# One reduction over four terms in place of three multiply-adds, in an RK4 step on one Trainium2 core

## The chip, the cores and the metric

The kernel runs on one core of a Trainium2 chip. The metric is the device time of one execution in microseconds. Three executions of the kernel before gave 6045.94, 6048.6 and 6047.53 us; their median, 6047.53 us, is the time before. TensorE multiplies matrices, VectorE (DVE in the profile) and ScalarE (ACT) work element by element on 128 partitions, GpSimd (POOL) only fills constants here, and SyncE (SP) issues the transfers. Each engine has its own queue of instructions and works through it in order; between engines, and for a result on the same engine, semaphores order the work.

## The reference

Two layers follow one another. The first is one attention head over `x` of shape (8, 512, 1024); it takes under a tenth of the time and the change doesn't touch it. The second integrates 512 time steps with the classical fourth-order Runge-Kutta scheme and adds the trace of `q` to its input:

```
def _derivative(q, p, drive, coupling, bias):
    i_couple = jnp.tanh(q) @ coupling.T
    dq = q - q ** 3 / 3.0 - p + drive + i_couple + bias
    dp = EPSILON * (q + ALPHA - BETA * p)
    return (dq, dp)

def _rk4_step(q, p, drive, coupling, bias):
    dq1, dp1 = _derivative(q, p, drive, coupling, bias)
    dq2, dp2 = _derivative(q + 0.5 * DT * dq1, p + 0.5 * DT * dp1, drive, coupling, bias)
    dq3, dp3 = _derivative(q + 0.5 * DT * dq2, p + 0.5 * DT * dp2, drive, coupling, bias)
    dq4, dp4 = _derivative(q + DT * dq3, p + DT * dp3, drive, coupling, bias)
    q_next = q + DT / 6.0 * (dq1 + 2 * dq2 + 2 * dq3 + dq4)
    p_next = p + DT / 6.0 * (dp1 + 2 * dp2 + 2 * dp3 + dp4)
    q_next = jnp.clip(q_next, -CLAMP, CLAMP)
    p_next = jnp.clip(p_next, -CLAMP, CLAMP)
    return (q_next, p_next)
...
drive_tbn = jnp.swapaxes(input_drive_seq, 0, 1)
```

The state `q` is 8 rows (batch) of 1024 values, the coupling is 1024 x 1024, and each of the 4 stages of a step needs the whole `q` of the stage before. So the second layer is a chain of 512 x 4 = 2048 stages, each with one product of an 8 x 1024 matrix by a 1024 x 1024 one.

## The kernel before

**Layout.** The 1024 values lie as 8 blocks of 128 partitions, so `q` is a tile of 128 x 64 (8 blocks times 8 rows of the batch). All tiles of the state are slices of one buffer, and the profile calls each of them `xb`. The blocks form two chunks: chunk 0 has 3 blocks (24 columns), chunk 1 has 5 (40 columns). The tanh and the coupling are each split into a high and a low half-precision part; the tanh's parts are called FIRST and REST. FIRST comes from a forecast or from the tanh itself, REST is what is missing from it.

**One stage.** A stage `s` goes round the engines in this order:

1. TensorE (line 604) multiplies, and its results lie in `ps`. It begins when FIRST and REST of chunk 0 are there (`first_ready[0]`, `rest_ready[0]`), and goes on to its second half when those of chunk 1 are. It signals `product_done[0]`, and after the last matmuls `product_done[1]`.
2. VectorE transposes the product of each chunk into `turned_sums` (`turn_product`, line 796; 96 columns for chunk 0, 160 for chunk 1).
3. VectorE adds the REST product to what was prepared (`q_of`): `q_next = turned_sum * step_scale + base`. `step_scale` is a column of one value for each partition, since the coupling was scaled by its own power of two.
4. ScalarE takes the tanh of that chunk (`tanh`, line 422), VectorE makes REST out of it (`rest_of`, seen as `tanh_parts<-xb,tanh_parts`), and TensorE starts the next stage.

**The prepared part.** `base` is made on VectorE between stages: `with_first_part` adds the product of FIRST, scaled by `step_scale`, to the linear terms; ScalarE squares the new `q` (line 466); `cubic_of` (line 819) makes `(q*q - 3) * q`; `base_of` adds that, scaled, to the rest.

**Order.** Nothing is scheduled by a program: `stage(s, now)` lists VectorE's instructions by hand, with the work for `p` and the linear terms placed between the links of the chain. Nearly all multiply-adds are made by one helper, `axpy`, and have its line, 646. In stage 0 and stage 2 ScalarE also forecasts the tanh of the stage after next (line 434, copied at line 440), and where the next stage is odd it copies the tanh to FIRST (line 428). VectorE's loop holds two steps, 8 stages, and branches back (line 1035) behind the last work of a stage 0. In stage 3, `clip_p` (914), `clip_q` (928) and `drive_less_p` (923) stand ahead of the second `rest_of`.

Of the kernel before, what the change touches and what calls it, by code (L numbers as in the profile page):

```python
# [17 lines left out]
P = 128  # L18
# [58 lines left out]
TANH_SCALE = 4096.0  # L77
COUP_EXP = 14
DRIVE_LOADS = 8
# [5 lines left out]
def build(nc, x, x_pt, cond, cond_p, wq, wk, wv, wo, coupling_t, bias_p, out_pt):  # L85
    ctx = ExitStack()
    with ctx:
# [18 lines left out]

        turned_sums = sb("turned_sums", [P, NC, SQ])
# [34 lines left out]
        step_scale = sb("step_scale", [P, STAGES])  # L142
# [13 lines left out]
        cubic = state()  # L156
        base = state()
        z = state()
        z2 = state()
        z3 = state()  # L160
        z_first_part = state()
# [17 lines left out]
        z_rest = state()  # L179

# [64 lines left out]
        cubic_ready = sem("cubic_ready")  # L245
        base_ready = sem("base_ready")

        z_ready = sem("z_ready")
        z_rest_ready = sem("z_rest_ready")
# [106 lines left out]
        def _(act):  # L356
# [68 lines left out]
            def first_part_as_now(parity, j, count):  # L425

                act.wait_ge(tanh_ready[j], count)
                nc.scalar.activation(tanh_part(parity, j, FIRST), by_block(tanh_sb, CHUNKS[j]), ACT.Copy,  # L428
                                     scale=TANH_SCALE).then_inc(first_ready[j], 1)

            def first_part_from_forecast(parity, factor, forecasts, made):

                act.wait_ge(forecast_ready, forecasts)
                nc.scalar.activation(tanh_hat[:, :], forecast[:, :], ACT.Tanh, scale=factor)\  # L434
# [4 lines left out]
                for j in range(NCH):  # L439
                    nc.scalar.activation(tanh_part(parity, j, FIRST), by_block(tanh_hat, CHUNKS[j]), ACT.Copy,  # L440
                                         scale=TANH_SCALE).then_inc(first_ready[j], 1)

            for j in range(NCH):
                tanh(q_st[0], j, 1)
            for j in range(NCH):
                act.wait_ge(tanh_ready[j], 1)
                nc.scalar.activation(tanh_part(1, j, FIRST), by_block(tanh_sb, CHUNKS[j]), ACT.Copy,
                                     scale=TANH_SCALE).then_inc(start_ready, 1)
            for j in range(NCH):
                first_part_as_now(0, j, 1)  # L450
            nc.scalar.activation(square[:, :], q_st[0][:, :], ACT.Square).then_inc(square_ready, 1)

            with act.Fori(1, 1 + STAGES * STEPS, STAGES * UNROLLED) as now:
                for u in range(STAGES * UNROLLED):
                    s = u % STAGES
                    following = (s + 1) % STAGES
                    parity = following % 2
                    made = act.snap(now + 1)
                    q = q_st[following] if following else q_raw
                    for j in range(NCH):  # L460
                        tanh(q, j, made)
                        if following % 2 == 1:
                            first_part_as_now(parity, j, made)
                    if following == 0:
                        act.wait_ge(clipped, act.snap(now >> 2))
# [175 lines left out]
        def _(dve):  # L641
# [98 lines left out]
            V.tensor_scalar(all_max[:, :], small_ps[:, 0:1], 2.0 ** -100, 2.0 ** 100, ALU.max, ALU.min)\  # L740
# [31 lines left out]
            V.tensor_copy(q_st[0][:, :], cond_sb[:, :, :].rearrange("p c b -> p (c b)"))  # L772
# [301 lines left out]
```

## Time and profile before

| | |
|---|---|
| median of three executions | 6047.53 us |
| the profiled execution | 6057.33 us, of which the span is 6055.5 us |
| VectorE busy | 5678.5 us, 94% of the span |
| TensorE busy (matmul) | 4516.8 us, 75% |
| ScalarE busy | 2596.6 us, 43% |
| mean granted TensorE clock | 0.995 of full speed |
| the 2048 stages | 430.5 us to the end |

A busy share counts the time in which at least one instruction of the engine is under way. Successive VectorE instructions overlap at their ends: one begins before the one ahead has written its last result. So a duration is one thing (when the result is there for another engine) and the distance from one start to the next is another (when the queue is free for the next). Both are used below. Starts stand in the timeline, to 0.01 us.

### The profile page before, as it was taken

To read this page: it belongs to the slowest core of one execution; us is meant where nothing else is said; L and a number is where in the kernel's file an instruction comes from. 1 tells how busy PE (TensorE), PEld (TensorE's weight loads), DVE (VectorE), ACT (ScalarE), POOL (GpSimd) and SP (SyncE) were. 2 spreads that over 40 slices of the span, in tenths; PEclk is the share of its full clock that TensorE was granted. 3 is DMA by queue.
4 is the path that set the end of the run, shared out by engine and by line. 5 is a ranking of instruction groups with operands and counts; after the bars stand their busy time and mean duration, and the time that the engine had idled before them with its cause. 6 is when DMAs were issued, how large, how long until landed. Compare 5 with 4: busy or idle time off the path is not lost.

```text
span 6055.5 us, 592967 instructions
## 1 busy us (share of the span) xinstructions
PE 4516.8 (75%) x263627; PEld 3815.0 (63%) x263627; DVE 5678.5 (94%) x32584; ACT 2596.6 (43%) x12040; POOL 5.6 (0%) x16
## 2 busy tenths in 40 slices
PE   7887777777777777777777777777777777777777
PEld 3446666666666666666666666666666666666666
DVE  5569999999999999999999999999999999999999
ACT  3334444444444444444444444444444444444444
POOL 0000000000000000000000000000000000000000
PEclk8999999999999999999999999999999999999999
DMA  5100000000000000000000000000000000000000
GB/s 206 44 15 0 0 7 0 7 0 7 0 0 7 0 7 0 7 0 0 7 0 7 0 7 0 0 7 0 7 0 7 0 0 7 0 7 0 7 0 7
DMA packets 11597, 57.06 MB, mean 9 GB/s; under 512 B 2616, under 2 KB 2616, under 8 KB 8512
## 3 DMA queue, kind: packets, MB, share of 16 engines
q1 hardware_dynamic: 11056, 55.84, 2.3%
q10 hardware_dynamic: 528, 1.05, 0.0%
q8 instruction: 7, 0.11, 0.0%
q14 instruction: 6, 0.05, 0.0%
HBM read 40.11 MB, written 16.78 MB: 9 GB/s over the span
## 4 chain that ended last, share of the span: by engine, by line
DVE 81%; issue 8%; ACT 5%; PE 5%; DVEq 1%; DMA 0%; SPq 0%; ACTq 0%
DVE xb L646 44%; DVE turned_sums L796 14%; DVE tanh_parts L646 8%; ACT xb L422 5%; DVE xb L819 5%; DVE xb L855 2%; DVE xb L923 2%; PE ps L493 2%; DVE drive L934 1%; DVE xb L908 1%; DVE xb L884 1%; PE ps L511 1%; DVE xb L914 1%; PE ps L548 1%; PE ps L537 1%
## 5 line engine op out<-in xcount | busy, mean ns | idle before, releaser
L604 PE MATMUL ps<-coup,tanh_parts 128*16 128x96 f16 (+1 forms) x262272 | 4165.0, 219 | 1463.9 <-ACT tanh_parts L428 740.9
L604 PEld LDWEIGHTS ps<-coup,tanh_parts 128*16 128x16 f16 x262272 | 3652.9, 89 | 1976.6 <-ACT tanh_parts L428 924.5
L422 ACT ACTIVATE xb<-xb 128x24 f32<-128x24 f32 (+1 forms) x4098 | 940.4, 230 | 3091.9 <-DVE xb L646 3081.7
L646 DVE SCALAR_TENSOR_TENSOR xb<-xb 128x64 f32<-128x64 f32 x11267 | 2153.5, 214 | 70.0
L646 DVE SCALAR_TENSOR_TENSOR xb<-turned_sums,step_scale,xb 128x64 f32<-128x64 f32 (+2 forms) x6145 | 1561.2, 261 | 41.7 <-issue 0.4
L796 DVE STREAM_TRANSPOSE turned_sums<-ps 128x96 f32<-128x96 f32 (+1 forms) x4096 | 1281.5, 313 | 70.4 <-issue 69.1
L646 DVE SCALAR_TENSOR_TENSOR tanh_parts<-xb,tanh_parts 128x24 f16<-128x24 f32 (+1 forms) x4098 | 717.1, 175 | 15.6
L466 ACT ACTIVATE xb<-xb 128x64 f32<-128x64 f32 x2048 | 499.3, 244 | 0.0
L428 ACT ACTIVATE tanh_parts<-xb 128x24 f16<-128x24 f32 (+1 forms) x2050 | 471.1, 230 | 64.5
L819 DVE SCALAR_TENSOR_TENSOR xb<-xb 128x64 f32<-128x64 f32 x2049 | 450.8, 220 | 0.1
L440 ACT ACTIVATE tanh_parts<-xb 128x24 f16<-128x24 f32 (+1 forms) x2048 | 357.3, 221 | 32.2
L434 ACT ACTIVATE xb<-xb 128x64 f32<-128x64 f32 x1024 | 263.4, 257 | 0.0
L855 DVE TENSOR_TENSOR xb<-xb 128x64 f32<-128x64 f32 x1024 | 225.9, 221 | 0.0
L392 ACT ACTIVATE probs<-ps,neg_max 128x1024 f32<-128x1024 f32 x64 | 71.3, 1115 | 147.4 <-DVE neg_max L661 147.4
L493 PE MATMUL ps<-k_aug,q_aug 128*128 128x512 f32 x256 | 126.4, 618 | 0.0
L646 DVE SCALAR_TENSOR_TENSOR drive<-ps,row_scale,drive 128x512 f32 (+1 forms) x64 | 84.3, 1349 | 43.6 <-PE ps L537 42.3
L471 ACT ACTIVATE xb<-xb 128x64 f32<-128x64 f32 x512 | 122.6, 240 | 0.0
L661 DVE TENSOR_REDUCE neg_max<-ps 128x1 f32<-128x1024 f32 x64 | 78.2, 1224 | 46.1 <-PE ps L493 46.1
L923 DVE TENSOR_TENSOR xb<-xb 128x64 f32<-128x64 f32 x512 | 115.5, 225 | 0.0
L884 DVE TENSOR_TENSOR xb<-drive 128x64 f32 x512 | 112.4, 219 | 0.0
L934 DVE TENSOR_TENSOR drive<-drive,xb 128x64 f32 x513 | 112.1, 218 | 0.0
L908 DVE TENSOR_TENSOR xb<-xb 128x64 f32<-128x64 f32 x512 | 112.0, 219 | 0.0
(69 smaller groups left out, 914.7 us busy)
## 6 DMA issues: line engine op xcount, KB each, us to landing
xb<-in_x SPq DMA_DIRECT2D x8, 2048.0 KB, 7.9
drive<-in_x_pt SPq DMA_DIRECT2D x8, 2048.0 KB, 24.5
out_pt<-drive SPq DMA_DIRECT2D x16, 1024.0 KB, 4.5
drive<-in_coupling_t SPq DMA_DIRECT2D x8, 512.0 KB, 11.5
mask_v<-in_cond SPq DMA_DIRECT2D x8, 132.0 KB
probs<-in_wo ACTq DMA_DIRECT2D x1, 1024.0 KB, 5.6
w_qkv<-in_wq SPq DMA_DIRECT2D x1, 64.0 KB, 3.8
w_qkv<-in_wk SPq DMA_DIRECT2D x1, 64.0 KB, 5.2
```

Of the source, the lines that this page charges most:

```text
L422: nc.scalar.activation(cols(tanh_sb, CHUNKS[j]), cols(q, CHUNKS[j]), ACT.Tanh)\
L428: nc.scalar.activation(tanh_part(parity, j, FIRST), by_block(tanh_sb, CHUNKS[j]), ACT.Copy, scale=TANH_SCALE).then_inc(first_ready[j], 1)
L434: nc.scalar.activation(tanh_hat[:, :], forecast[:, :], ACT.Tanh, scale=factor)\
L440: nc.scalar.activation(tanh_part(parity, j, FIRST), by_block(tanh_hat, CHUNKS[j]), ACT.Copy, scale=TANH_SCALE).then_inc(first_ready[j], 1)
L466: nc.scalar.activation(square[:, :], q_st[following][:, :], ACT.Square).then_inc(square_ready, 1)
L493: last = nc.tensor.matmul(score_ps[t % 2][:, BANK * h:BANK * (h + 1)], q_aug[:, P * t:P * (t + 1)], k_aug[:, BANK * h:BANK * (h + 1)], sta ...
L604: last = nc.tensor.matmul(product(s, j)[SQ * g:SQ * g + ROWS, :], tanh_parts[:, s % 2, k, :], coup[:, k, part, g, n0:n1, :].rearrange("p c ...
L646: return V.scalar_tensor_tensor(out=out, in0=a, scalar=factor, in1=c, op0=ALU.mult, op1=op1)
L796: V.transpose(turned_sums[:, CHUNKS[j][0]:CHUNKS[j][1], :].rearrange("p c r -> p (c r)"), product(s, j)).then_inc(product_turned[j], 1)
L819: V.scalar_tensor_tensor(out=cubic[:, :], in0=square[:, :], scalar=-3.0, in1=q_st[stage][:, :], op0=ALU.add, op1=ALU.mult)\
L855: V.tensor_tensor(rise[stage - 1][:, :], q_st[stage][:, :], q_st[0][:, :], ALU.subtract)
L923: V.tensor_tensor(drive_p[:, :], drive_b[:, :], p_st[:, :], ALU.subtract)\
```

## The change

All of `q`'s quantities (`q`, `p`, drive, bias) are now held divided by `rho`, a power of two that is worked out from the coupling at run time. In this unit a product of FIRST or REST is a term of `q` as it is, with no factor. A new tile area `terms` holds for each of the 8 blocks 168 columns: the transposed products (32), the linear part (8) and the curve part (8), twice, for even and odd stages. `q_of` is now one `tensor_reduce` with add over four 8-column pieces: linear, curve, FIRST product and REST product. Its input is a view of four dimensions (`c b i j`, summed over `i` and `j`), whose two inner steps are 80 columns and 24 or 40 columns.

`with_first_part` and `base_of` are gone. ScalarE makes a new tile `slope`, `q` times a constant, behind each square, so that `curve_of` needs one instruction. The constants that depended on the unit become columns of one value for each partition: the scale of the tanh, the square and the forecast's tanh (`rho`, `factors`), both bounds of both clips (`limits`), and a factor in `trace`, `look_ahead` and `less_q_of`.

```
-TANH_SCALE = 4096.0
+TANH_EXP = 20
+STATE_EXP = COUP_EXP + TANH_EXP
+TANH_SCALE = [step * 2.0 ** TANH_EXP for step in STEP]
+TURNED = [0, 32]
+LINEAR = [88, 80]
+CURVE = [112, 120]
+SPREAD = [24, 40]
+PAIRS = 80
+TERMS = 168
...
+        def summands(s, j):
+            lowest = 8 if s % 2 == 0 else 0
+            pairs = terms[:, CHUNKS[j][0]:CHUNKS[j][1], lowest:lowest + 2 * PAIRS].rearrange("p c (i x) -> p c i x", i=2)
+            pairs = pairs[:, :, :, 0:2 * SPREAD[s % 2]].rearrange("p c i (j y) -> p c i j y", j=2)
+            return pairs[:, :, :, :, 0:B].rearrange("p c i j b -> p c b i j")
...
-                nc.scalar.activation(cols(tanh_sb, CHUNKS[j]), cols(q, CHUNKS[j]), ACT.Tanh)\
-                  .then_inc(tanh_ready[j], 1)
+                nc.scalar.activation(cols(tanh_sb, CHUNKS[j]), cols(q, CHUNKS[j]), ACT.Tanh,
+                                     scale=rho[:, 0:1]).then_inc(tanh_ready[j], 1)
...
+            def square_and_slope(stage):
+                nc.scalar.activation(square[:, :], q_st[stage][:, :], ACT.Square, scale=rho[:, 0:1])
+                nc.scalar.activation(slope[:, :], q_st[stage][:, :], ACT.Copy, scale=-STEP[stage] / 3)\
+                  .then_inc(square_ready, 1)
...
                 dve.wait_ge(product_turned[j], now)
                 out = q_st[s + 1] if s + 1 < STAGES else q_raw
-                axpy(by_block(out, CHUNKS[j]), turned_sum(j, REST), step_scale[:, s:s + 1],
-                     by_block(base, CHUNKS[j])).then_inc(q_next[j], 1)
+                V.tensor_reduce(by_block(out, CHUNKS[j]), summands(s, j), AX.XY, ALU.add).then_inc(q_next[j], 1)
...
-                V.scalar_tensor_tensor(out=cubic[:, :], in0=square[:, :], scalar=-3.0,
-                                       in1=q_st[stage][:, :], op0=ALU.add, op1=ALU.mult)\
-                 .then_inc(cubic_ready, 1)
-
-            def base_of(stage, made):
-
-                dve.wait_ge(cubic_ready, made)
-                axpy(base[:, :], cubic[:, :], -STEP[stage] / 3, z_first_part[:, :]).then_inc(base_ready, 1)
+                V.scalar_tensor_tensor(out=curve(stage), in0=all_blocks(square), scalar=-3.0,
+                                       in1=all_blocks(slope), op0=ALU.add, op1=ALU.mult)\
+                 .then_inc(curve_ready, 1)
...
-                V.tensor_scalar(p_st[:, :], p_raw[:, :], -CLAMP - SHIFT, CLAMP - SHIFT, ALU.max, ALU.min)\
+                V.tensor_scalar(p_st[:, :], p_raw[:, :], limits[:, 2:3], limits[:, 3:4], ALU.max, ALU.min)\
                  .then_inc(p_ready, STAGES)
```

In VectorE's queue, this is the beginning of stage 2 before, from its first transpose to the second `rest_of` and the forecast behind it:

```order
L796 STREAM_TRANSPOSE turned_sums<-ps 128x96
L646 SCALAR_TENSOR_TENSOR xb<-xb 128x64
L646 SCALAR_TENSOR_TENSOR xb<-turned_sums,step_scale,xb 128x24
L646 SCALAR_TENSOR_TENSOR xb<-xb 128x64
L796 STREAM_TRANSPOSE turned_sums<-ps 128x160
L646 SCALAR_TENSOR_TENSOR tanh_parts<-xb,tanh_parts 128x3x8
L646 SCALAR_TENSOR_TENSOR xb<-turned_sums,step_scale,xb 128x40
L646 SCALAR_TENSOR_TENSOR xb<-turned_sums,step_scale,xb 128x64
L934 ISA
L934 TENSOR_TENSOR drive<-drive,xb 128x64
L646 SCALAR_TENSOR_TENSOR tanh_parts<-xb,tanh_parts 128x5x8
```

And this is the same place of the changed kernel (`L675` is now the helper's line, `L840` the reduction's):

```order
L830 STREAM_TRANSPOSE xb<-ps 128x3x32
L675 SCALAR_TENSOR_TENSOR xb<-xb 128x64
L840 TENSOR_REDUCE xb<-xb 128x24
L675 SCALAR_TENSOR_TENSOR xb<-xb 128x64
L830 STREAM_TRANSPOSE xb<-ps 128x5x32
L675 SCALAR_TENSOR_TENSOR tanh_parts<-xb,tanh_parts 128x3x8
L840 TENSOR_REDUCE xb<-xb 128x40
L675 ISA
L675 SCALAR_TENSOR_TENSOR drive<-xb,rho,drive 128x64
L675 SCALAR_TENSOR_TENSOR tanh_parts<-xb,tanh_parts 128x5x8
```

Both `q_of` have become reductions, and the `with_first_part` behind the second is gone. The links of the chain stand in the same order.

In ScalarE's queue, before, the work that follows a `q` whose stage is odd:

```order
L422 ACTIVATE xb<-xb 128x24
L428 ACTIVATE tanh_parts<-xb 128x3x8
L422 ACTIVATE xb<-xb 128x40
L428 ACTIVATE tanh_parts<-xb 128x5x8
L466 ACTIVATE xb<-xb 128x64
L433 REGISTER_ALU
L434 ACTIVATE xb<-xb 128x64
```

and now:

```order
L445 ACTIVATE xb<-xb,rho 128x24
L451 ACTIVATE tanh_parts<-xb 128x3x8
L445 ACTIVATE xb<-xb,rho 128x40
L451 ACTIVATE tanh_parts<-xb 128x5x8
L477 ACTIVATE xb<-xb,rho 128x64
L478 ACTIVATE xb<-xb 128x64
L456 REGISTER_ALU
L457 ACTIVATE xb<-xb,factors 128x64
```

Both tanh, the square and the forecast's tanh read a column as their scale, and one instruction (478, `slope`) stands behind the square.

## Rows read from the trace of the kernel before

**Rows 1.** The page: busy time and share of each engine, instructions.

```profile
PE 4516.8 (75%) x263627; PEld 3815.0 (63%) x263627; DVE 5678.5 (94%) x32584; ACT 2596.6 (43%) x12040; POOL 5.6 (0%) x16
```

**Rows 2.** Line 796: duration in ns (min/median/max), first and last start.

```profile
L796 DVE STREAM_TRANSPOSE turned_sums<-ps x4096: 274/313/351, 430.5 to 6048.8; 128x96 f32<-128x96 f32 x98, 128x160 f32<-128x160 f32 x98
```

**Rows 3.** Timeline of VectorE in a stage 2: start us, duration us, instruction.

```profile
3005.69 0.28 DVE L796 STREAM_TRANSPOSE turned_sums<-ps 128x96 f32<-128x96 f32 x1
...
3006.09 0.24 DVE L646 SCALAR_TENSOR_TENSOR xb<-turned_sums,step_scale,xb 128x24 f32<-128x24 f32 x1
3006.25 0.22 DVE L646 SCALAR_TENSOR_TENSOR xb<-xb 128x64 f32<-128x64 f32 x1
3006.38 0.34 DVE L796 STREAM_TRANSPOSE turned_sums<-ps 128x160 f32<-128x160 f32 x1
3006.65 0.15 DVE L646 SCALAR_TENSOR_TENSOR tanh_parts<-xb,tanh_parts 128x24 f16<-128x24 f32 x1
3006.76 0.45 DVE L646 SCALAR_TENSOR_TENSOR xb<-turned_sums,step_scale,xb 128x40 f32<-128x40 f32 x2
...
3007.32 0.20 DVE L646 SCALAR_TENSOR_TENSOR tanh_parts<-xb,tanh_parts 128x40 f16<-128x40 f32 x1
...
3007.85 0.22 DVE L819 SCALAR_TENSOR_TENSOR xb<-xb 128x64 f32<-128x64 f32 x1
3008.10 0.23 DVE L646 SCALAR_TENSOR_TENSOR xb<-xb 128x64 f32<-128x64 f32 x1
3008.32 0.28 DVE L796 STREAM_TRANSPOSE turned_sums<-ps 128x96 f32<-128x96 f32 x1
```

**Rows 4.** Timeline of ScalarE in the same stage.

```profile
3006.36 0.22 ACT L422 ACTIVATE xb<-xb 128x24 f32<-128x24 f32 x1 [1.68 <-DVE xb L646]
...
3007.05 0.24 ACT L422 ACTIVATE xb<-xb 128x40 f32<-128x40 f32 x1 [0.21 <-DVE xb L646]
3007.32 0.24 ACT L428 ACTIVATE tanh_parts<-xb 128x40 f16<-128x40 f32 x1
3007.46 0.24 ACT L466 ACTIVATE xb<-xb 128x64 f32<-128x64 f32 x1
```

**Rows 5.** Timeline of VectorE at the loop's branch, behind a stage 0.

```profile
3002.43 0.23 DVE L646 SCALAR_TENSOR_TENSOR xb<-xb 128x64 f32<-128x64 f32 x1
3002.93 0.28 DVE L796 STREAM_TRANSPOSE turned_sums<-ps 128x96 f32<-128x96 f32 x1 [0.27 <-issue]
```

**Rows 6.** Groups by line: VectorE's small reductions (busy us, mean ns of one).

```profile
L651 DVE TENSOR_REDUCE v_sb<-stack 128x32 f32<-128x128 f32 x4 | 1.2, 362 | 2.2 <-POOL stack L344 2.2
L734 DVE TENSOR_REDUCE all_max<-col_max 128x1 f32<-128x8 f32 x1 | 0.2, 161 | 0.0
```

**Rows 7.** Timeline of VectorE at the start: the four reductions of line 651.

```profile
2.22 1.20 DVE L651 TENSOR_REDUCE v_sb<-stack 128x32 f32<-128x128 f32 x4 [2.22 <-POOL stack L344]
```

**Rows 8.** Timeline of VectorE in stage 3, from the second `q_of`.

```profile
3009.40 0.26 DVE L646 SCALAR_TENSOR_TENSOR xb<-turned_sums,step_scale,xb 128x40 f32<-128x40 f32 x1
3009.57 0.19 DVE L914 TENSOR_SCALAR xb<-xb 128x64 f32<-128x64 f32 x1
3009.69 0.20 DVE L928 TENSOR_SCALAR xb<-xb 128x64 f32<-128x64 f32 x1
3009.87 0.23 DVE L923 TENSOR_TENSOR xb<-xb 128x64 f32<-128x64 f32 x1
3010.01 0.19 DVE L646 SCALAR_TENSOR_TENSOR tanh_parts<-xb,tanh_parts 128x40 f16<-128x40 f32 x1
```

**Rows 9.** Groups by line: ScalarE with and without a column operand.

```profile
L392 ACT ACTIVATE probs<-ps,neg_max 128x1024 f32<-128x1024 f32 x64 | 71.3, 1115 | 147.4 <-DVE neg_max L661 147.4
L373 ACT ACTIVATE q_aug<-ps 32x1024 f32<-32x1024 f32 x8 | 8.2, 1021 | 39.6 <-PE ps L548 39.6
L411 ACT ACTIVATE coup<-drive,coup_scale 128x256 f16<-128x256 f32 x32 | 12.9, 496 | 4.7 <-DVE coup_scale L748 4.7
```

**Rows 10.** Groups by line: VectorE's `tensor_scalar` with and without a column operand.

```profile
L777 DVE TENSOR_SCALAR xb<-xb,bias_sb 128x8 f32<-128x8 f32 x8 | 1.2, 227 | 0.0
L751 DVE TENSOR_SCALAR step_scale<-power 128x1 f32<-128x1 f32 x4 | 0.3, 144 | 0.0
```

More of the change, by code:

```diff
@@ L155, in build @@
         square0 = state()
[L156 to L161, printed above, removed]
+        slope = state()
         forecast = state()
@@ L179, in build @@
         z_rest = state()
+        first = next(states)
+        terms = xb[:, :, :].rearrange("p c n -> p (c n)")[:, first:first + NC * TERMS]\
+            .rearrange("p (c k) -> p c k", k=TERMS)
         ps = ctx.enter_context(nc.psum_tensor("ps", [P, NBANK, BANK], F32))
@@ L439, in first_part_from_forecast @@
                 for j in range(NCH):
[L440 to L441 removed]
+                    nc.scalar.activation(tanh_part((stage + 1) % 2, j, FIRST), by_block(tanh_hat, CHUNKS[j]), ACT.Copy,
+                                         scale=TANH_SCALE[stage]).then_inc(first_ready[j], 1)
             for j in range(NCH):
@@ L780, in _ @@
             dve.wait_ge(setup, 6)
-            for j in range(NCH):
-                V.engine_nop().then_inc(q_next[j], 1)
-            V.tensor_tensor(drive_b[:, :], steps[:, 0, :], bias_b[:, :], ALU.add).then_inc(setup, 1)
+            V.tensor_scalar(bias_b[:, :], y[:, :], inv_rho[:, 0:1], None, ALU.mult).then_inc(setup, 1)
             dve.wait_ge(setup, 7)
+            axpy(drive_b[:, :], steps[:, 0, :], inv_rho[:, 0:1], bias_b[:, :]).then_inc(setup, 1)
+            dve.wait_ge(setup, 8)
             V.tensor_tensor(drive_p[:, :], drive_b[:, :], p_st[:, :], ALU.subtract).then_inc(setup, 1)
@@ L941, in _ @@
                 rest_of(0, j, 1)
-            cubic_of(0, 1)
             dve.wait_ge(start_done, 1)
             for j in range(NCH):
-                last = V.transpose(turned_sums[:, CHUNKS[j][0]:CHUNKS[j][1], :].rearrange("p c r -> p (c r)"),
-                                   product(1, j))
+                last = V.transpose(turned_product(1, j), product(1, j).rearrange("p (c r) -> p c r", r=SQ))
             last.then_inc(start_turned, 1)
-            dve.wait_ge(setup, 9)
             dve.wait_ge(start_turned, 1)
-            with_first_part(0, z_first_part, z).then_inc(setup, 1)
-            dve.wait_ge(setup, 10)
-            base_of(0, 1)
             g0_of()
+            curve_of(0, 1)
             def stage(s, now):
                 following = (s + 1) % STAGES
-                parity = following % 2
                 made = after(now)
@@ L968, in stage @@
                 if s == 3:
-                    p_next()
+                    look_ahead((now + STAGES) * (COLS // STAGES))
                 q_of(s, 0, now)
@@ L977, in stage @@
                 if s == 3:
-                    look_ahead((now + STAGES) * (COLS // STAGES))
+                    p_next()
                 turn_product(s, 1, now)
-                rest_of(parity, 0, made)
+                rest_of(following, 0, made)
                 q_of(s, 1, now)
@@ L987, in stage @@
                     p_sum_r(1)
-                    drive_step_of((now + 2) * (COLS // STAGES))
                 if s == 2:
-                    with_first_part(3, z_rest, z_rest).then_inc(z_rest_ready, STAGES)
                     trace((now - 3) * (COLS // STAGES))
```

140 lines of the change are left out of this document (71 added, 69 removed).

## The prediction

> **What bounds the kernel now.** I read the page first, then where the stages lie in time, then the timelines of VectorE and ScalarE over single stages, and last the groups by line for instructions like the new ones. VectorE is busy 94% of the span and TensorE 75% [rows 1], which looks as if VectorE's queue were the bound and each instruction fewer a gain. The stages say how far that goes. The first transpose starts at 430.5 us and the last at 6048.8 [rows 2]; the last is that of chunk 1, 0.69 us behind its stage's first (3005.69 to 3006.38 [rows 3]), so 2047 stages take 5617.6 us: 2.744 us each, 10.98 us a step.
>
> The stage 2 in [rows 3] takes 3005.69 to 3008.32, 2.63 us, and its end isn't set by VectorE's queue: the last instruction ahead of the next transpose starts at 3008.10, and the transpose 0.22 us later, where such an instruction otherwise frees the queue after 0.13 (3006.25 to 3006.38). The 0.09 us between are a wait for the product. So here the walk round the engines binds, with VectorE's queue only in places on it. Call the first transpose 0. `q_of` of chunk 0 starts at 0.40, the second transpose at 0.69, `rest_of` of chunk 0 at 0.96, `q_of` of chunk 1 at 1.07. The tanh of chunk 1 starts at 1.36 and takes 0.24 [rows 4], its `rest_of` starts at 1.63, and 1.00 us later the product is there and the next transpose starts at 2.63. That is the floor of a stage; the mean of 2.744 is only 0.11 us above it. The queue's own work explains that excess, the loop's branch most plainly: 0.50 us from the last instruction to the transpose [rows 5]. So taking work off VectorE can give at most 0.11 us a stage, and anything that makes the walk longer costs at once.
>
> **What is removed.** Each stage loses `with_first_part` and `base_of`, 8 instructions of 63 a step. `base_of` waits for `cubic_of`: 3007.85 to 3008.10 is 0.25 us [rows 3], where the queue alone would need 0.13. All this lies behind the second `rest_of`, where VectorE has 1.00 us while TensorE multiplies. Taken off the queue it is worth about 0.45 us (0.25, and some 0.20 for a multiply-add with a column: one over 24 columns frees the queue after 0.16, 3006.09 to 3006.25 [rows 3]), but only down to the floor: from 2.744 to 2.63, 0.11 x 2048 = 235 us at most.
>
> **What is added on the walk.** Three things, all between the first transpose and the second `rest_of`.
>
> *The reductions.* No row has this one; the nearest is line 651, which also sums four values a pitch apart, 128 elements to 32: 362 ns each [rows 6], and four take 1.20 us [rows 7], so the queue is free after (1.20 - 0.36)/3 = 0.28 us. A reduction of 8 elements to 1 takes 161 ns [rows 6]. At one element in 1.04 ns (as 24 columns to 40 of the same multiply-add go from 0.24 to 0.26 [rows 3, 8]) the fixed part is 153 ns, so line 651 pays 362 - 153 - 133 = 76 ns more, for its pitch or for its 32 results; both scale alike here. For 96 elements to 24: 153 + 100 + 57 = 0.31 us, free after 0.23. For 160 to 40: 153 + 167 + 95 = 0.41 us, free after 0.33. `q_of` took 0.24 and 0.26 and freed the queue after 0.16 [rows 3, 8]. The lower end is no extra for pitch or results: 0.25 and 0.32 us, free after 0.17. Upward I see no row that binds: a view of four dimensions may cost more than line 651's two; I allow 0.1 us on each. I take line 651, as it is the only one with a pitch.
>
> *The scale of the tanh as a column.* The exponential with a column as bias takes 1115 ns for 1024 elements, the copy without one 1021 [rows 9]: 0.09 us. Line 411, with a column as scale, takes 496 ns for 256; a copy of 64 takes 240 [rows 4], and 192 more elements at 0.84 to 1.04 ns bring 400 to 440, so 0.06 to 0.10. I take 0.09 for each tanh. The lower end is 0, if the exponential's extra is for something else.
>
> *The walk with these.* `q_of` 0 at 0.40, done at 0.71. Its tanh starts at 0.74, takes 0.31, and `rest_of` 0 starts at 1.08 (by the queue alone 0.40 + 0.23 + 0.13 + 0.27 = 1.03, so the tanh now decides). `q_of` 1 at 1.19, done at 1.60; tanh 1.63, takes 0.33; `rest_of` 1 at 1.99. The matmuls are the same, so + 1.00 gives 2.99 us, against 2.63.
>
> **What else could set a stage's end.** *Square and slope.* Where the next stage is odd, ScalarE does tanh, copy, square: 0.27 and 0.14 us apart [rows 4], now 0.36 and 0.14. The square starts at 2.13, with its column passes on after 0.24, and the slope is done at 2.61; `curve_of` starts at 2.64 instead of behind the queue. The transpose is due at 2.99, so it is covered, except at the branch: 2.64 + 0.50 = 3.14, which is 0.15 over, once in two steps: 0.07 us a step. *Stage 1* has a wait for the curve and two instructions behind it: there the slope is done at 2.35, the curve starts at 2.38, + 0.25 + 0.14 + 0.20 = 2.97, just covered. *Stage 3* has the clips ahead of `rest_of` 1. They stand 0.12 and 0.18 us apart [rows 8] with bounds as constants. A `tensor_scalar` with a column takes 227 ns for 8 elements, one without 144 for 1 [rows 10]: 0.075 us for a column, so 0.07 to 0.15 us for two. From `q_of` 1 at 1.19 + 0.33 = 1.52: `clip_p` to 1.70 to 1.77, `drive_less_p` at 1.89 to 2.02, + 0.14 is 2.03 to 2.16 against 1.99. I take 0.10 us a step. *Columns in `trace`, `look_ahead`, `less_q_of`*: some 0.07 us of queue each, `look_ahead` inside the 0.40 us to the first `q_of`, `trace` inside the wait for the tanh, `less_q_of` counted above: nothing. If that cover were gone, 0.2 us a step. *Ahead of the loop* there are some ten instructions more, of 0.06 to 0.2 us once: nothing.
>
> **The sum.** 4 x 2.99 + 0.07 + 0.10 = 12.13 us a step, against 10.98: + 1.15 us, x 512 = + 589 us. The profiled execution took 6057.33 us (its span 6055.5 and 1.8 around it) and would take 6646; it lies 9.8 us, 0.16%, above the median of the runs, so for the median 6637. I say 6640 us, 9.8% slower.
>
> **A rule against the row.** The timeline shows a walk round the engines with 0.09 us of VectorE's queue idle in front of a product [rows 3]. The Trainium skill, "VectorE: DVE Perf Modes", section "Rules for kernel authors", says for chained work to minimize the count of operations, and in the same table that `tensor_reduce` is the slowest VectorE operation and one should restructure around it. By the first the change gains, by the second it loses; the trace bears out the second as far as line 651 goes. The first, as a mechanism of this kernel, is the second rival below.
>
> **The rivals.**
>
> *The reductions are cheap (0.12).* No extra for pitch or results. For it: no row separates the extra of line 651 from something else. Against: 76 ns are measured. Walk: `rest_of` 0 at 1.02, `q_of` 1 at 1.13, done 1.45, `rest_of` 1 at 1.84, stage 2.84. 4 x 2.84 + 0.17 = 11.53, + 0.55 x 512 = + 283: 6330 us.
>
> *Fewer instructions win (0.04), the other side.* VectorE's queue is what counts and the reductions are no dearer than `q_of` was, nor the tanh with a column, because their latency is hidden. The stage falls to the floor: 2.63 x 4 = 10.52, - 0.46 x 512 = - 235: 5812 us. For it: the 94% and the branch. The point from which it decides: later release by `q_of` 0, longer `q_of` 1 and longer tanh together under 0.11 us a stage, less what stage 3 adds; my rows give 0.36.
>
> *The tanh's column is free (0.08).* Then `rest_of` 0 is at 1.03, `q_of` 1 done at 1.55, `rest_of` 1 at 1.86, stage 2.86; the branch adds 0.03 and stage 3 now 0.20, since its tanh no longer covers the clips. 11.67, + 0.69 x 512 = + 353: 6400 us. Against: the two rows agree on 0.06 to 0.10.
>
> *The reductions are dearer than line 651 (0.15).* 0.1 us each, in duration and release: both lie on the walk, 0.20 us a stage, 0.8 a step, + 410: 7050 us. For it: the view has four dimensions with two inner steps.
>
> **How the numbers follow.** My forecast has 0.60, the rivals 0.12, 0.04, 0.08 and 0.15, no change 0.01. Slower by over 0.2% (about what a measurement of this kernel can tell from none) is all but two of these: 0.95; faster 0.04, same 0.01. The forecast's own spread, by 0.03 us on a reduction or on the clips, is some 60 to 120 us each way. The range of 6370 to 6880 holds it, the free column and the lower half of the dearer reductions, and leaves out the cheap reductions and the far ends.
>
> **What the profile after would show.** The first transposes 3.0 us apart; VectorE's busy share well down, with idle time ahead of the first transpose put down to TensorE, and ahead of `rest_of` to ScalarE; reductions of 0.31 and 0.41 us; tanh of 0.31 and 0.33; 1.00 us from the second `rest_of` to the transpose unchanged; stage 3 the longest but for the branch's. The prediction is wrong if the reductions take under 0.3 us or over 0.5, if the tanh still takes 0.24, or if the part from `rest_of` to the transpose is not 1.00, since the matmuls aren't touched.

## The result, and the profile after

The changed kernel takes 6657.17 us (median of four executions, 6656.35 to 6660.73), the kernel before 6048.07 us beside it on the same chip (6045.94 to 6049.23). The ratio is 1.1009, with a 95% interval of 1.099 to 1.1028: 609 us or 10.1% slower. The prediction said 6640 us.

The page of the changed kernel, its busy times and its chain that ended last:

```profile
PE 4733.9 (71%) x263627; PEld 3813.4 (57%) x263627; DVE 5804.1 (87%) x28492; ACT 3456.6 (52%) x14089; POOL 5.6 (0%) x16
...
DVE 50%; PE 26%; ACT 12%; issue 11%; DMA 1%; DVEq 0%; SPq 0%; ACTq 0%
```

VectorE has 4092 instructions fewer than in [rows 1] and is yet busy for 126 us more, since the new ones are longer. Its share falls from 94% to 87%: what was added is mostly waiting. The chain that ended last says the same: in the page of before, 81% of it is VectorE and 5% TensorE, here it is 50% and 26%. The matmuls are the same in number, and the groups of both kernels have them at the same 206 and 233 ns each; TensorE's 217 us more of busy time are therefore not more work. In after_split and before_cover, below, the figure is 4508 and 4507 us, as before; in the four kernels with a reduction that are below it is 4708 to 4739, and in split_all_const, with the same matmuls again, 4398. What makes it differ is open.

The transposes' line, which answers to [rows 2] (duration in ns, first and last start):

```profile
L830 DVE STREAM_TRANSPOSE xb<-ps x4096: 282/310/351, 426.3 to 6647.9; 128x96 f32<-128x96 f32 x98, 128x160 f32<-128x160 f32 x98
```

The last is the second of its stage, 0.75 us behind the first. So 2047 stages take 6647.9 - 0.75 - 426.3 = 6220.85 us: 3.039 us each, where before had 2.744; 12.16 us a step, where the sum of the prediction had 12.13.

A stage 2 in VectorE's timeline, which answers to [rows 3]:

```profile
3010.03 0.28 DVE L830 STREAM_TRANSPOSE xb<-ps 128x96 f32<-128x96 f32 x1
...
3010.41 0.32 DVE L840 TENSOR_REDUCE xb<-xb 128x24 f32<-128x96 f32 x1
3010.65 0.22 DVE L675 SCALAR_TENSOR_TENSOR xb<-xb 128x64 f32<-128x64 f32 x1
3010.78 0.35 DVE L830 STREAM_TRANSPOSE xb<-ps 128x160 f32<-128x160 f32 x1
3011.12 0.18 DVE L675 SCALAR_TENSOR_TENSOR tanh_parts<-xb,tanh_parts 128x24 f16<-128x24 f32 x1
3011.22 0.42 DVE L840 TENSOR_REDUCE xb<-xb 128x40 f32<-128x160 f32 x1
3011.56 0.28 DVE L675 SCALAR_TENSOR_TENSOR drive<-xb,rho,drive 128x64 f32 x1
3012.03 0.20 DVE L675 SCALAR_TENSOR_TENSOR tanh_parts<-xb,tanh_parts 128x40 f16<-128x40 f32 x1 [0.20 <-ACT xb L445]
...
3012.69 0.23 DVE L853 SCALAR_TENSOR_TENSOR xb<-xb 128x64 f32<-128x64 f32 x1
3013.03 0.28 DVE L830 STREAM_TRANSPOSE xb<-ps 128x96 f32<-128x96 f32 x1
```

Counted from the first transpose, the links start at (before, forecast, measured): `rest_of` of chunk 0 0.96, 1.08, 1.09; second `q_of` 1.07, 1.19, 1.19; second `rest_of` 1.63, 1.99, 2.00; next transpose 2.63, 2.99, 3.00. The second `rest_of` now stands behind 0.20 us of idle queue that the trace puts to the tanh, and the last instruction ahead of the transpose begins 0.34 us before it, where a queue that sets the time would need 0.13.

The groups of the loop, by form, between 400 and 6500 us (busy us, mean ns of one):

```profile
L840 DVE TENSOR_REDUCE xb<-xb 128x40 f32<-128x160 f32 x1999 | 837.3, 419 | 0.0
L445 ACT ACTIVATE xb<-xb,rho 128x40 f32<-128x40 f32 x1999 | 655.0, 328 | 918.1 <-DVE xb L840 918.1
L840 DVE TENSOR_REDUCE xb<-xb 128x24 f32<-128x96 f32 x1999 | 637.5, 319 | 0.0
L445 ACT ACTIVATE xb<-xb,rho 128x24 f32<-128x24 f32 x2000 | 627.9, 314 | 1789.3 <-DVE xb L840 1780.2 <-DVEq L814 9.1
```

The reductions take 319 and 419 ns (forecast 0.31 and 0.41 us), the tanh 314 and 328 (forecast 0.31 and 0.33).

### The profile page after: what moved, and what is told of

It reads as the page before. It is cut to its first block, busy times and chain, and to the rows that moved or that the text cites. A ratio compares the mean times of both kernels' runs of the same rounds, so it can differ in the third digit from the quotient of the medians.

```text
span 6654.7 us, 590410 instructions
## 1 busy us (share of the span) xinstructions
PE 4733.9 (71%) x263627; PEld 3813.4 (57%) x263627; DVE 5804.1 (87%) x28492; ACT 3456.6 (52%) x14089; POOL 5.6 (0%) x16
## 4 chain that ended last, share of the span: by engine, by line
DVE 50%; PE 26%; ACT 12%; issue 11%; DMA 1%; DVEq 0%; SPq 0%; ACTq 0%
PE ps L633 22%; DVE xb L840 16%; DVE xb L830 13%; ACT xb L445 8%; DVE xb L675 7%; DVE tanh_parts L675 5%; ACT tanh_parts L451 3%; DVE xb L938 2%; DVE xb L947 2%; DVE xb L853 1%; DVE xb L908 1%; PE ps L522 1%; DVE xb L880 1%; ACT xb L477 1%; ACT xb L478 1%
## 5 line engine op out<-in xcount | busy, mean ns | idle before, releaser
L633 PE MATMUL ps<-coup,tanh_parts 128*16 128x96 f16 (+1 forms) x262272 | 4387.7, 219 | 1843.6 <-DVE tanh_parts L675 917.1
L445 ACT ACTIVATE xb<-xb,rho 128x24 f32<-128x24 f32 (+1 forms) x4098 | 1314.5, 321 | 2773.4 <-DVE xb L840 2764.3
L675 DVE SCALAR_TENSOR_TENSOR xb<-xb 128x64 f32<-128x64 f32 x8706 | 1671.6, 211 | 17.6
L830 DVE STREAM_TRANSPOSE xb<-ps 128x96 f32<-128x96 f32 (+1 forms) x4096 | 1280.9, 313 | 290.4 <-PE ps L633 200.0
L840 DVE TENSOR_REDUCE xb<-xb 128x24 f32<-128x96 f32 (+1 forms) x4096 | 1510.9, 369 | 0.0
L675 DVE SCALAR_TENSOR_TENSOR tanh_parts<-xb,tanh_parts 128x24 f16<-128x24 f32 (+1 forms) x4098 | 780.2, 190 | 232.2 <-ACT xb L445 102.5
L477 ACT ACTIVATE xb<-xb,rho 128x64 f32<-128x64 f32 x2049 | 688.7, 336 | 60.5
L853 DVE SCALAR_TENSOR_TENSOR xb<-xb 128x64 f32<-128x64 f32 x2049 | 459.3, 224 | 135.6 <-ACT xb L478 93.5
L478 ACT ACTIVATE xb<-xb 128x64 f32<-128x64 f32 x2049 | 491.7, 240 | 0.0
L457 ACT ACTIVATE xb<-xb,factors 128x64 f32<-128x64 f32 x1024 | 340.9, 333 | 0.0
L880 DVE TENSOR_TENSOR xb<-xb 128x64 f32<-128x64 f32 x1024 | 223.0, 218 | 0.0
L952 DVE TENSOR_SCALAR xb<-xb,limits 128x64 f32<-128x64 f32 x512 | 157.6, 308 | 0.0
L938 DVE TENSOR_SCALAR xb<-xb,limits 128x64 f32<-128x64 f32 x512 | 155.6, 304 | 0.0
L675 DVE SCALAR_TENSOR_TENSOR xb<-xb,factors 128x64 f32<-128x64 f32 x512 | 141.9, 277 | 0.0
L675 DVE SCALAR_TENSOR_TENSOR drive<-xb,rho,drive 128x64 f32 x513 | 141.3, 275 | 0.0
L675 DVE SCALAR_TENSOR_TENSOR xb<-drive,inv_rho,xb 128x64 f32<-128x64 f32 x513 | 125.0, 244 | 0.0
L500 ACT ACTIVATE xb<-xb 128x64 f32<-128x64 f32 x512 | 123.0, 240 | 0.0
```

The lines of the kernel that those rows point to most:

```text
L477: nc.scalar.activation(square[:, :], q_st[stage][:, :], ACT.Square, scale=rho[:, 0:1])
L478: nc.scalar.activation(slope[:, :], q_st[stage][:, :], ACT.Copy, scale=-STEP[stage] / 3)\
L633: last = nc.tensor.matmul(product(s, j)[SQ * g:SQ * g + ROWS, :], tanh_parts[:, s % 2, k, :], coup[:, k, part, g, n0:n1, :].rearrange("p c ...
L675: return V.scalar_tensor_tensor(out=out, in0=a, scalar=factor, in1=c, op0=ALU.mult, op1=op1)
L830: V.transpose(turned_product(s, j), product(s, j).rearrange("p (c r) -> p c r", r=SQ))\
L840: V.tensor_reduce(by_block(out, CHUNKS[j]), summands(s, j), AX.XY, ALU.add).then_inc(q_next[j], 1)
```

## The experiments

Each kernel was timed beside the kernel before on its chip, where that took 6054 to 6055 us; the changed kernel would take 1.1009 times as much there, some 6666 us, and that is what the losses below are counted against. The intervals of the ratios are 0.002 wide to each side, so such a difference is good to some 15 us.

### probe: what the instructions cost

The kernel before, with groups of five like instructions behind the last stage, on a scratch tile.

```
+            for i in range(5):
+                V.tensor_reduce(out_blocks(5, i), four(5), AX.XY, ALU.add)
+            for i in range(5):
+                V.tensor_reduce(to(40, i), adjacent, AX.X, ALU.add)
...
+            for i in range(5):
+                nc.scalar.activation(fill(), fa[:, 0:40], ACT.Tanh)
+            for i in range(5):
+                nc.scalar.activation(fill(), fa[:, 0:40], ACT.Tanh, scale=power[:, 0:1])
```

> The kernel before, with groups of five like instructions behind its last stage, on VectorE and on ScalarE, each on scratch data. If a reduction is dear for its pitch, 160 elements to 40 take about 0.32 us where the four values lie side by side and about 0.41 us where they lie a pitch apart. If it is dear for the number of its results, both take 0.41 us, and 160 elements to 1 take 0.32. The view of four dimensions takes 0.31 (96 to 24) and 0.41 us (160 to 40) by both. A tanh of 40 elements takes 0.24 us with a constant scale and 0.33 with a column; with two columns 0.42 if each is charged. A tensor_scalar of 64 elements takes 0.19 us with two constants, 0.26 with one column, and 0.26 or 0.33 with two.

The groups at the end (busy us, mean ns of one). Line 1089 sums four values 8 columns apart, 1083 and 1085 are the change's own view, 1087 and 1095 have the values side by side (1095 makes one result); 485 has a column as scale, 487 one as bias, 489 both; 1105 and 1107 have one and two columns:

```profile
L1089 DVE TENSOR_REDUCE probs_t<-probs_t 128x40 f32<-128x160 f32 x5 | 1.8, 438 | 0.0
...
L1085 DVE TENSOR_REDUCE probs_t<-probs_t 128x40 f32<-128x160 f32 x5 | 1.7, 422 | 0.0
...
L489 ACT ACTIVATE probs<-probs,inv_power,power 128x40 f32<-128x40 f32 x5 | 1.7, 407 | 0.0
...
L1087 DVE TENSOR_REDUCE probs_t<-probs_t 128x40 f32<-128x160 f32 x5 | 1.2, 324 | 0.0
L1095 DVE TENSOR_REDUCE probs_t<-probs_t 128x1 f32<-128x160 f32 x5 | 1.2, 318 | 0.0
...
L1107 DVE TENSOR_SCALAR probs_t<-probs_t,step_scale 128x64 f32<-128x64 f32 x5 | 1.2, 318 | 0.0
L1083 DVE TENSOR_REDUCE probs_t<-probs_t 128x24 f32<-128x96 f32 x5 | 1.2, 305 | 0.0
L487 ACT ACTIVATE probs<-probs,power 128x40 f32<-128x40 f32 x5 | 1.2, 313 | 0.0
L485 ACT ACTIVATE probs<-probs,power 128x40 f32<-128x40 f32 x5 | 1.2, 313 | 0.0
...
L1105 DVE TENSOR_SCALAR probs_t<-probs_t,step_scale 128x64 f32<-128x64 f32 x5 | 0.9, 257 | 0.0
```

This settles what the prediction left open ("for its pitch or for its 32 results"). With the values side by side, one result costs as much as forty: 318 against 324 ns. With the values apart it is 422 to 438, whether by 8 columns or in the change's four dimensions. So the extra of 98 to 114 ns for 160 elements goes with the pitch alone, and the two inner steps that the dearer rival rested on cost nothing of their own. A column adds 91 ns to ScalarE's 222 (group of line 483) and 60 to VectorE's 197 (line 1103), each further one as much again.

### after_tanh_const: the column of the tanh

```
-                                     scale=rho[:, 0:1]).then_inc(tanh_ready[j], 1)
+                                     scale=2.0 ** (-5 - STATE_EXP)).then_inc(tanh_ready[j], 1)
```

The constant is `rho`'s value for this coupling.

> The changed kernel with the tanh's scale as a constant in place of the column rho; the constant is the value that rho has for this coupling. If the column lies on the walk round the engines as the prediction has it, a stage falls from 2.99 to 2.86 us and the time to about 6400 us (6360 to 6450). If ScalarE's extra is hidden, because the next rest_of waits for VectorE's queue anyway, it stays at 6657.

Measured: 6427.02 us, ratio 1.0613 (1.0595 to 1.0631). One operand of the 4096 tanh instructions costs 239 us. In VectorE's timeline of a stage 2:

```profile
3011.97 0.28 DVE L830 STREAM_TRANSPOSE xb<-ps 128x96 f32<-128x96 f32 x1
...
3012.36 0.32 DVE L840 TENSOR_REDUCE xb<-xb 128x24 f32<-128x96 f32 x1
...
3012.99 0.16 DVE L675 SCALAR_TENSOR_TENSOR tanh_parts<-xb,tanh_parts 128x24 f16<-128x24 f32 x1
3013.11 0.43 DVE L840 TENSOR_REDUCE xb<-xb 128x40 f32<-128x160 f32 x1
...
3013.84 0.20 DVE L675 SCALAR_TENSOR_TENSOR tanh_parts<-xb,tanh_parts 128x40 f16<-128x40 f32 x1
...
3014.84 0.28 DVE L830 STREAM_TRANSPOSE xb<-ps 128x96 f32<-128x96 f32 x1
```

The stage has 2.87 us. The second `rest_of` comes 0.73 us behind its `q_of` instead of 0.81, and that `q_of` starts at 1.14 instead of 1.19, the rest of the gain: the first `rest_of`, behind the shorter tanh, now waits for the second transpose in its queue (it starts 0.27 behind it) and no longer for the tanh. That is the walk which the prediction gave for a free column (2.86), so the trace and the sum agree.

### after_adjacent: the pitch of the reduction

```
-            lowest = 8 if s % 2 == 0 else 0
-            pairs = terms[:, CHUNKS[j][0]:CHUNKS[j][1], lowest:lowest + 2 * PAIRS].rearrange("p c (i x) -> p c i x", i=2)
-            pairs = pairs[:, :, :, 0:2 * SPREAD[s % 2]].rearrange("p c i (j y) -> p c i j y", j=2)
-            return pairs[:, :, :, :, 0:B].rearrange("p c i j b -> p c b i j")
+            own = terms[:, CHUNKS[j][0]:CHUNKS[j][1], TURNED[s % 2]:TURNED[s % 2] + SQ]
+            return own.rearrange("p c (b k) -> p c b k", k=4)
```

> The changed kernel with each reduction over four values side by side inside the transposed product, in place of the linear, curve and product pieces (so q is another sum; work, sizes and waits are the same). If the pitch is what a reduction is dear for, the two take 0.25 and 0.32 us, a stage falls to 2.84 us and the time to about 6340 us (6300 to 6400). If the number of results is, it stays within 0.5% of 6657.

Measured: 6312.28 us, ratio 1.0423 (1.0406 to 1.0441). The groups of the reduction:

```profile
L838 DVE TENSOR_REDUCE xb<-xb 128x40 f32<-128x160 f32 x2045 | 638.3, 312 | 0.0
L838 DVE TENSOR_REDUCE xb<-xb 128x24 f32<-128x96 f32 x2045 | 517.4, 253 | 0.0
```

This kernel sums other values, so its `q` is another. The reductions have as many elements and as many results as in the changed kernel and are 107 and 66 ns shorter. The time falls by 354 us, 0.173 us a stage, as 107 + 66 = 173 ns would have it: both lie on the walk in full.

### after_split: the reduction taken apart again

The unit of `q` and all columns stay as in the change; the FIRST product and the linear part are summed ahead (`with_first_part`), the curve added to that (`base_of`), and `q_of` adds the REST product with one `tensor_tensor`.

```
-                V.tensor_reduce(by_block(out, CHUNKS[j]), summands(s, j), AX.XY, ALU.add).then_inc(q_next[j], 1)
+                at = TURNED[s % 2] + B * REST
+                V.tensor_tensor(by_block(out, CHUNKS[j]), terms[:, CHUNKS[j][0]:CHUNKS[j][1], at:at + B],
+                                by_block(base, CHUNKS[j]), ALU.add).then_inc(q_next[j], 1)
```

> The changed kernel with the one reduction taken apart again: FIRST's product is added to the linear part and the curve to that behind the second rest_of, and q is one tensor_tensor of REST's product and this base. The unit and all columns stay. If the reductions on the walk are the larger part of the loss, as the prediction has it, stages are 2.67 to 2.90 us, 11.18 us a step, and the time is about 6160 us (6090 to 6230). If the loss is the unit's columns, it stays over 6450 us. If VectorE's queue were the bound, eight instructions more a step would make it slower than 6657.

Measured: 6175.06 us, ratio 1.0197 (1.018 to 1.0214), so 491 us go with the reduction: that is what it costs against a sum taken apart, although the latter has 8 instructions a step more in the queue. 354 of them are the pitch (after_adjacent). The transposes' line:

```profile
L835 DVE STREAM_TRANSPOSE xb<-ps x4096: 272/312/351, 428.3 to 6167.3; 128x96 f32<-128x96 f32 x98, 128x160 f32<-128x160 f32 x98
```

With the second transpose 0.69 us behind the first, that makes 2.803 us a stage.

### after_extra_pair: is the work that was removed worth anything?

Two multiply-adds into unused tiles, in stages 0, 2 and 3, where `with_first_part` and `base_of` stood.

```
+            def extra_pair():
+                axpy(unused[0][:, :], bias_b[:, :], DT, bias_b[:, :])
+                axpy(unused[1][:, :], bias_b[:, :], DT, bias_b[:, :])
```

> The changed kernel with two unused multiply-adds of 64 elements put in where with_first_part and base_of stood, in stages 0, 2 and 3: six instructions more a step on VectorE, 0.8 us of its queue. If the walk sets the stages, all of it lies in the time in which VectorE waits for the product, and the ratio to the kernel before stays at 1.101 within 0.003. If VectorE's queue still set them, it would be 0.8 x 512 = 415 us, a ratio of 1.17.

Measured: 6663.01 us, ratio 1.1005 (1.099 to 1.102). The change's ratio is 1.1009, so six instructions a step more cost nothing that can be measured. Stage 1 got no pair, so for it this run says nothing. A stage 3 with them:

```profile
3007.20 0.28 DVE L831 STREAM_TRANSPOSE xb<-ps 128x96 f32<-128x96 f32 x1
...
3009.31 0.19 DVE L676 SCALAR_TENSOR_TENSOR tanh_parts<-xb,tanh_parts 128x40 f16<-128x40 f32 x1
3009.43 0.63 DVE L676 SCALAR_TENSOR_TENSOR xb<-xb 128x64 f32<-128x64 f32 x4
3009.97 0.22 DVE L854 SCALAR_TENSOR_TENSOR xb<-xb 128x64 f32<-128x64 f32 x1
3010.30 0.28 DVE L831 STREAM_TRANSPOSE xb<-ps 128x96 f32<-128x96 f32 x1
```

Four instead of two stand behind the second `rest_of`, and still 0.33 us pass between the last one's start and the transpose. The stage has 3.10 us, as the change's stage 3 has. VectorE's share is up from 87% to 91%, and the time is the same. So in these three stages the queue isn't the bound of the changed kernel, and the rival that fewer instructions win is refuted.

### after_all_const and split_all_const: all columns of the loop

All operands that are columns in the loop (tanh, square, forecast, clips, `trace`, `look_ahead`, `less_q_of`) become constants, once in the changed kernel and once in after_split. The constants hold for couplings whose largest entry is at least 1/32 and under 1/16, as this one's is.

```
-                V.tensor_scalar(p_st[:, :], p_raw[:, :], limits[:, 2:3], limits[:, 3:4], ALU.max, ALU.min)\
+                V.tensor_scalar(p_st[:, :], p_raw[:, :], (-CLAMP - SHIFT) * 2.0 ** (5 + STATE_EXP), (CLAMP - SHIFT) * 2.0 ** (5 + STATE_EXP), ALU.max, ALU.min)\
```

> The changed kernel with every column of the loop (tanh, square, forecast, clips, trace, look_ahead, less_q_of) as a constant of this coupling's value. The prediction charged the columns outside the tanh to stage 3 (the clips) and to the branch alone: then a step is 11.49 us against 11.67 with the tanh's alone, and the time about 6335 us (6290 to 6380). If the clips' columns are hidden, it stays at the 6427 of the run with the tanh's constant.

> The kernel with the reduction taken apart again (after_split) and every column of the loop as a constant. Neither of the two costs on the walk is left, and q is a tensor_tensor with no column. By the walk the floor of a stage is 2.51 us; VectorE's queue gives 2.66, 2.70, 2.56 and 2.55 us for stages 0 to 3, 10.47 us a step, and a time of about 5790 us (5720 to 5870), faster than the kernel before. If the unit itself costs something beyond its columns (the slope on ScalarE), it stays over 5950.

Measured: 6327.32 us (ratio 1.045, 1.0434 to 1.0466) and 5855.33 us (0.9672, 0.9658 to 0.9687). All columns cost the changed kernel some 339 us, of which the tanh's are 239. Without columns and without the reduction the new unit is 3.3% faster than before. Gone through in this order, the loss of 609 us is some 491 for the reduction (after_split) and 318 for the columns that are left in after_split, less 199 that the unit brings (split_all_const). `q_of` then needs no factor: it takes 0.18 and 0.20 us where before, with `step_scale` as a column, it took 0.24 and 0.26 [rows 3, 8], and it stands on the walk twice a stage. How much of the 3.3% is this, and how much `base_of` and the others without a factor, no run separates.

The expectation for split_all_const was 65 us too low. In VectorE's timeline of it:

```profile
3000.51 0.28 DVE L835 STREAM_TRANSPOSE xb<-ps 128x96 f32<-128x96 f32 x1
3000.70 0.18 DVE L680 SCALAR_TENSOR_TENSOR xb<-xb 128x64 f32<-128x64 f32 x1
3000.89 0.18 DVE L846 TENSOR_TENSOR xb<-xb 128x24 f32<-128x24 f32 x1
3000.99 0.22 DVE L680 SCALAR_TENSOR_TENSOR xb<-xb 128x64 f32<-128x64 f32 x1
3001.19 0.35 DVE L835 STREAM_TRANSPOSE xb<-ps 128x160 f32<-128x160 f32 x1
...
3003.08 0.28 DVE L835 STREAM_TRANSPOSE xb<-ps 128x96 f32<-128x96 f32 x1
```

The second transpose comes 0.20 us behind the instruction ahead of it, not 0.13. I had moved it up with the shorter `q_of` in every stage, but here it stays at 0.68 behind the first, 0.69 in [rows 3]. The same timeline with TensorE's matmuls (merged by the view: start, then the time to the end of the last, which is modelled) shows why, for a stage 1 and the stage 2 behind it:

```profile
3002.81 0.91 PE L638 MATMUL ps<-coup,tanh_parts 128*16 128x96 f16 x44
3003.77 0.35 DVE L835 STREAM_TRANSPOSE xb<-ps 128x160 f32<-128x160 f32 x1
...
3004.33 1.97 PE L638 MATMUL ps<-coup,tanh_parts 128*16 128x96 f16 x128 [0.61 <-DVE tanh_parts L680]
3006.47 0.34 DVE L835 STREAM_TRANSPOSE xb<-ps 128x160 f32<-128x160 f32 x1
```

In the stage 1 the product of chunk 1 ends at 3003.72 and its transpose starts 0.05 us later, 0.69 behind the first (3003.08). In the stage 2 it ends at 3006.30, and the transpose starts 0.17 us later, where VectorE's queue lets it, 0.62 behind the first (3005.85). Over the whole loop it starts 0.05 us behind the last matmul of chunk 1 in both stages 0 and in one of the two stages 1 (at 0.68 to 0.69), and in stage 3 (at 0.64). In the others the product is there earlier, and the transpose starts at 0.62, as 0.13 behind the instruction ahead of it has it. So I had the second transpose up to 0.07 us too early: 0.065 us in stage 0, 0.034 in the mean of stage 1 and 0.025 in stage 3, 0.124 us a step, make 64 us, which is nearly all that the expectation lacked. The stage shown first has 2.57 us.

### before_cover and before_cover_unroll4: the excess of before over its floor

The prediction says that before has 0.11 us a stage over its floor of 2.63, and that the queue's own work makes it. before_cover keeps before's arithmetic and only moves instructions: at least one that waits for nothing stands between `cubic_of` and `base_of` in each stage, `drive_step_of` goes to a stage 0, in stages 1 and 3 two pairs of instructions, and behind the second `rest_of` some single ones, change places, and `turned_sums` lies in the area of `xb` (so the profile names it `xb`). The second kernel also holds four steps in the loop instead of two (`UNROLLED = 4`).

```
                     rise_of(1)
+                    drive_step_of((now + 3) * (COLS // STAGES))
...
-                    base_of(2, made)
...
+                    base_of(2, made)
```

> The kernel before, its arithmetic unchanged, with one independent instruction between cubic_of and base_of in each stage, so that base_of doesn't wait 0.12 us for its input. If VectorE's queue sets stages 0, 1 and 3 and the walk stage 2, the stages are 2.63 (2.98 at the branch), 2.64, 2.63 and 2.73 us, 10.80 us a step, 1.5% faster than before (1% to 2%). If the queue alone counted, four waits of 0.12 us a step would give 4%. If the walk set every stage, nothing.

> The kernel of before_cover with four steps in a turn of the loop in place of two. The branch costs a stage 0.35 us over the walk, once in four steps: 45 us less than before_cover, 2.3% faster than before. If longer code of the loop makes instructions late, slower than before_cover.

Measured: 5936.8 us (0.9807, 0.9794 to 0.9821) and 5923.22 us (0.9783, 0.977 to 0.9797). So 118 us of the 235 that the removed work could at most bring are to be had without removing any. By stages (means over the loop), some 67 of them come from stage 1 (2.77 to 2.64 us) and 34 from the stage with the branch (2.96 to 2.83); stage 2 gives 7 back. The other 25 are no cover: in before, the second stage 0 of the loop takes 2.72 us because its first `q_of` starts 0.1 us late, at 0.48 behind the transpose, and here it starts at 0.39 and the stage takes 2.62. Why it was late is open (see below).

What is left stands in two places of the loop. Stage 3 takes 2.75 us (first transposes at 3003.82 and 3006.57), as in before: its second `rest_of` starts at 1.69, behind the clips, instead of 1.63, so half of its 0.12 over the floor is on the walk and no order of the work behind it brings it back. And the stage 0 with the branch takes 2.82 (3006.57 to 3009.39), where the other stage 0 takes 2.62. I had expected 2.98 there, and 1.5% instead of 1.9% for the whole.

The branch of before_cover, to be read beside [rows 5]:

```profile
3009.05 0.22 DVE L647 SCALAR_TENSOR_TENSOR xb<-xb 128x64 f32<-128x64 f32 x1
3009.39 0.28 DVE L797 STREAM_TRANSPOSE xb<-ps 128x96 f32<-128x96 f32 x1
```

From the last instruction to the transpose it is 0.34 us, where before took 0.50. There the last instruction, `base_of`, waited for `cubic_of`; here its input is long ready. What the branch itself does in that time no trace here shows.

With the branch once in four steps I expected 45 us less and got 14. The 45 were counted with a branch that costs its stage 0.35 us, as in before. In before_cover it costs 0.21 (2.83 against 2.62 us, means over the loop), which makes 26 us, and 12 of them are lost elsewhere: in before_cover_unroll4, in one stage 3 of the four steps of the loop,

```profile
3031.56 0.28 DVE L797 STREAM_TRANSPOSE xb<-ps 128x96 f32<-128x96 f32 x1
3031.77 0.18 DVE L920 TENSOR_TENSOR xb<-drive,xb 128x64 f32<-128x64 f32 x1
3032.06 0.24 DVE L647 SCALAR_TENSOR_TENSOR xb<-xb,step_scale 128x24 f32<-128x24 f32 x1
```

`q_of` starts 0.50 us behind the transpose, where 0.40 is the rule, with no wait shown. The kernel before has the same at one place of its loop (0.48). Both places are late in every pass. Why is open.

## Why the prediction was right

**What bounds.** That the walk binds in the changed kernel, though the page of before has VectorE at 94%, is shown by after_extra_pair from one side (more queue work costs nothing) and by after_adjacent from the other (173 ns off the walk give 173 ns a stage).

**The removed work** was put at 0.11 us a stage at most, and at nothing once the walk is longer. It is worth nothing in the changed kernel (1.1005 against 1.1009). In before the excess is real: 118 us of its 235 go in before_cover. That the queue's own work explains all of it was too simple: 0.06 us of stage 3 are the clips on the walk, and 0.1 us in one stage 0 of the loop is a late `q_of`, whose cause is open. Nor does all that was removed lie behind the second `rest_of`: in stage 2 the `with_first_part` stood ahead of it, inside the wait for the tanh. Neither moves the sum.

**The reductions** were sized from line 651 at 0.31 and 0.41 us and measured 0.319 and 0.419; the queue is free after 0.24 and 0.34 (3010.41 to 3010.65, 3011.22 to 3011.56), where I had 0.23 and 0.33. That line 651 pays for its pitch or for its results was left open, and the sum came out right because both scale alike; the probe says that it is the pitch. The lower end "no extra for pitch or results" was a real possibility that the rows could not exclude, and it is false: after_adjacent is 354 us faster. So is "0.1 us each" for four dimensions, which cost none.

**The columns.** 0.09 us for a tanh was right (91 ns). By the Trainium skill, "ScalarE: Activation LUTs", section "What ACT_TABLE_LOAD costs", each such operand adds about 93 ns; the probe's 222, 313 and 407 ns agree, for a scale as for a bias. The free column, 6400 us, is what after_tanh_const shows as a kernel: 6427.

**The rule.** The Trainium skill, "VectorE: DVE Perf Modes", section "Rules for kernel authors", gave two advices that point apart here. For this chain the one on `tensor_reduce` decides. The one on the count of operations has a limit, which the trace showed: an instruction that is covered by the wait for the product is worth nothing, and one on the walk counts with its full duration.

**Stage by stage.** Forecast 2.99 for a plain stage, 3.14 at the branch, 3.09 for stage 3; the first transposes stand 3.00, 3.15 (3003.89 to 3007.04) and 3.10 apart (3000.79 to 3003.89); the means over the loop are 3.00, 3.15 and 3.09. VectorE's timeline at the branch:

```profile
3003.89 0.28 DVE L830 STREAM_TRANSPOSE xb<-ps 128x96 f32<-128x96 f32 x1 [0.25 <-PE ps L633]
...
3006.54 0.22 DVE L853 SCALAR_TENSOR_TENSOR xb<-xb 128x64 f32<-128x64 f32 x1 [0.18 <-ACT xb L478]
3007.04 0.28 DVE L830 STREAM_TRANSPOSE xb<-ps 128x96 f32<-128x96 f32 x1 [0.27 <-PE ps L633]
```

`curve_of` waits for the slope until 2.65 (forecast 2.64), and the transpose follows 0.50 us later, as in [rows 5]. The trace puts the 0.27 us of idle time to TensorE, but a plain stage has its product at 3.00 and this one starts at 3.15: the label names the last semaphore, and the branch sets the time.

**What was off.** 12.16 us a step against 12.13, and 609 us against 589. In the profiled executions the loop is 603 us longer (6220.85 against 5617.6), 14 more than forecast; plain stages and the branch are each up to 0.01 above it. What stands ahead of the loop is 4 us shorter, where the sum had nothing (426.3 against 430.5). The other 10 us are not of the kernel. The prediction took off 9.8 us because the profiled execution of before lay that far above its median; that of the changed kernel lay 0.7 us below its own. By the profiled executions alone it is 599 us against 589.

## What to carry to other kernels

Before instructions are merged, find the walk of dependent results from one stage's start to the next, and price each link by its full duration, operands and access pattern included; instructions that end inside a wait are free, and what is saved there brings nothing. A sum over several operands that lie apart is cheap to write as one reduction, but it puts all terms behind the last one to arrive; adding early what is early, with one short operation for the late term, is the faster form here by 491 us. A run-time constant as a column costs on each instruction of the walk. Here the new unit takes a column off the two `q_of` and puts columns on both tanh and on the clips: with them it is 2.0% slower than before (after_split), with constants in their place 3.3% faster (split_all_const).

## What was not expected of the hardware

- A reduction over values a pitch apart costs 422 to 438 ns where one over adjacent values costs 324, 0.6 to 0.7 ns more for each element, at a pitch of 8 columns of 4 bytes as in the four-dimensional view with its steps of 24 to 80. With adjacent values the number of results doesn't matter (1 or 40); with a pitch no run varied it for the same elements.
- From the start of the last instruction ahead of the loop's branch to the start of the next behind it, it is 0.34 us where the last one's input is long ready, and 0.50 where it waited: for a result of the same engine in before, for ScalarE's slope in the changed kernel.
- In five of the eight stages of split_all_const's loop, VectorE's transpose of the second product starts 0.05 us behind the modelled end of that product's last matmul.
- An instruction at one place of an unrolled loop starts 0.1 us late in every pass, with no wait that the trace shows, in the kernel before and in the reordered one.
